# The order of VectorE's steps in the cross-attention of a perceiver kernel, and who adds up the last block's exponentials

## The chip, the cores and the metric

One core of one Trainium2 chip runs the whole program. The time is device microseconds (us) from one execution. Before the change the median of three runs is 1887.72 us, with 1887.4 as the lowest and 1889.46 as the highest.

The engines that matter here are TensorE (PE in the profile, with PEld for its weight loads), VectorE (DVE), ScalarE (ACT), GpSimd (POOL) and SyncE, which issues the DMAs. Each runs its own list of instructions in order and waits on semaphores for the others.

## The reference, cut to what matters

Three residual stages work on x (16 batches of 64 rows of 512). The change touches only the first, the cross-attention with a context of 1601 rows per batch:

```python
q = _split_heads(x @ Wq)            # 16 heads of 32, x after a layer norm
k = _split_heads(y @ Wk)            # y: 16 x 1601 x 512
v = _split_heads(y @ Wv)
attn = jnp.einsum('bhid,bhjd->bhij', q, k) * SCALE
attn = jax.nn.softmax(attn, axis=-1)
out = jnp.einsum('bhij,bhjd->bhid', attn, v)
x = x + out.transpose(0, 2, 1, 3).reshape(b, n, h * d) @ Wp + bp
```

A self-attention and a feed-forward stage follow; neither is changed.

## The kernel before, in words

The cross-attention runs batch by batch: batch 0 written out, batches 1 to 14 in a hardware loop on every engine, batch 15 written out. A batch has a keys phase and a values phase. The 16 heads are four blocks (NBLK) of four heads. Every product of float32 numbers is made in three passes over a high and a low part (three_passes, L113), 12 matmuls each.

**TensorE, keys phase** (batch(), from L942). For each block i it makes four pieces of keys, keys(b, i, 0) to (b, i, 3), and between them the scores of block i - 1 (L916). It also finishes the batch before: weigh(b - 1, i) multiplies that batch's exponentials with its values (L934, 104 small matmuls into small_ps) and spreads the sums of the exponentials by four heads x two halves of matmuls with ones (L938). The single bank small_ps holds one block at a time, so small_read(b - 1, i - 1) makes weigh(b - 1, i) wait until VectorE's output(b - 1, i - 1) has read the block before it.

**TensorE, values phase**. It makes twelve tiles of values, values(b, 0) to values(b, 11), and the scores of block 3 after the first two. Keys and values leave through three PSUM banks in turn (ring). ScalarE empties all key pieces and the odd value tiles, VectorE the even ones (value(b, t), L703). values(b, t) needs the bank of tile t - 3, so tiles 3, 5, 7, 9 and 11 wait for VectorE's copies 0, 2, 4, 6 and 8, and the first key piece of the next batch for copy 10.

**VectorE** (keys_phase, values_phase, L787 to L842) has for each block: largest(b, i, 0) and (b, i, 1), the maxima over the tiles of scores (L724 to L735); row_of_peaks(b, i), twelve small operations in a row that turn them into a row of maxima (L746 to L760); subtract(b, i), which takes that row from the scores in three pieces (L766). Between them stand output(b - 1, i) (a reciprocal at L771 and a product at L775), the copies value(b, t), and low(b + 1, q), the low parts of the next batch's context (L784).

**ScalarE** copies scores out of PSUM (L600), takes the exponentials in three pieces (L606) once subtract has signalled them, and makes the high parts of the context. **GpSimd** adds the 13 tiles of exponentials of a block one after the other (totals, L549 and L555, 12 additions); weigh waits for the last of them (sum_step) ahead of L938.

**Batch 0** has a third part between keys and values. The last 65 context rows of all 16 batches are gathered into nine tiles (LT), whose values TensorE makes at once (left_values(j)). For each tile ScalarE makes a high part (left_high), VectorE a low part (left_low, L707), and the result is copied out by VectorE for even j (left_value, L713) and by ScalarE for odd j. Three slots (LEFT_SLOTS) hold the parts, so the fourth tile waits for left_low(3).

**After batch 15** TensorE weighs its four blocks in banks of their own, with the first output products (out_ahead) between them, and then the block of code ends with a barrier.

Of the kernel before, what the change touches and what calls it, by code (L numbers as in the profile page):

```python
# [13 lines left out]
H, DH = 16, 32  # L14
# [32 lines left out]
TREE_N = 7  # L47
SQ = 32
ROW_N = 9
PIECES = ((0, 4), (4, 8), (8, JT))  # L50
SUMS = JT - 1
LAST_V = (3, 6, 9, VT - 1)
# [341 lines left out]
def cross_attention(nc, x, yT, y_left, v_left, q_dram, o_dram, wv, wp, bp, awq, sh, ident, ones, s_ps):  # L394
# [10 lines left out]
    with ctx:  # L405
# [47 lines left out]
        def last_bank(i):  # L453

            return ring[i] if i < RING else small_ps
# [84 lines left out]

        @block.gpsimd
        def _(pool):
            def totals(b, i):

                done, at = len(PIECES) * (NBLK * b + i), SUMS * (NBLK * b + i)
                acc = fold[:, i, :]
                pool.wait_ge(fold_read, NBLK * b + i + 1)
                pool.wait_ge(exp_ok, done + 1)
                pool.tensor_tensor(acc, prob[:, i, 0, :], prob[:, i, 1, :], ALU.add).then_inc(sum_step, 1)  # L549
                for t in range(2, JT):  # L550
                    if t in (PIECES[1][0], PIECES[2][0]):
                        pool.wait_ge(exp_ok, done + 2 + (t == PIECES[2][0]))
                    pool.wait_ge(sum_step, at + t - 1)
                    m = jtile(t)
                    pool.tensor_tensor(acc[0:m], acc[0:m], prob[0:m, i, t, :], ALU.add).then_inc(sum_step, 1)  # L555

            with pool.Fori(0, B) as b:
                for i in range(NBLK):
                    totals(b, i)
            pool.wait_ge(x_in, 32)  # L560
            for t in range(BIASED):
                if t == ROWS_AHEAD:
                    pool.wait_ge(x_late, 16)
                rows = y.w_raw if t < ROWS_AHEAD else x_rows
                pool.tensor_tensor(rows[:, t, :], rows[:, t, :], y.w_raw[:, ROWS_AHEAD, :], ALU.add)
# [130 lines left out]
        def _(dve):  # L696
# [90 lines left out]
            def keys_phase(b, past):  # L787
                if past:
                    output(b - 1, 0)
                else:  # L790
                    dve.wait_ge(wv_hi, 1)
                    dve.tensor_tensor(sh.wv_s[:, 1], wv_raw, sh.wv_s[:, 0].bitcast(F32),
                                      ALU.subtract).then_inc(wv_lo, 1)
                largest(b, 0, 0)
                largest(b, 0, 1)
                for i in (1, 2):
                    row_of_peaks(b, i - 1)
                    subtract(b, i - 1)
                    largest(b, i, 0)
                    if past:  # L800
                        output(b - 1, i)
                    elif i == 1:
                        for j in range(LEFT_SLOTS):
                            left_low(j)
                    largest(b, i, 1)
                if past:
                    output(b - 1, 3)
                row_of_peaks(b, 2)
                subtract(b, 2)
                if not past:  # L810
                    for j in range(LT):
                        if j % 2 == 0:
                            left_value(j)
                        if j + LEFT_SLOTS < LT:
                            left_low(j + LEFT_SLOTS)

            def values_phase(b, more):
                value(b, 0)
                largest(b, 3, 0)
                value(b, 2)  # L820
                largest(b, 3, 1)
                row_of_peaks(b, 3)
                value(b, 4)
                subtract(b, 3)
                if more:
                    low(b + 1, 0)
                value(b, 6)
                value(b, 8)
                if more:
                    low(b + 1, 1)  # L830
                else:
                    dve.wait_ge(wp_hi, 1)
                    dve.tensor_tensor(y.keep[:, 1], y.w_raw, y.keep[:, 0].bitcast(F32),
                                      ALU.subtract).then_inc(wp_lo, 1)
                    gather(0)
                value(b, 10)
                if more:
                    low(b + 1, 2)
                if more:
                    low(b + 1, 3)  # L840
                else:
                    gather(1)  # L842
# [20 lines left out]
        def _(pe):  # L863
# [57 lines left out]

                reached(pe, o_out, NBLK * b + i + 1)

            def weigh(b, i, at=small_ps):
                block = NBLK * b + i
                if i == 0:
                    pe.wait_ge(act_out, ACT_N * (b + 1))
# [3 lines left out]
                for t in range(JT):  # L931
                    m = jtile(t)
                    for g in range(HB):
                        pe.matmul(at[g * DH:(g + 1) * DH, 0:N], v_sb[0:m, t, (HB * i + g) * DH:(HB * i + g + 1) * DH],  # L934
                                  prob[0:m, i, t, g * N:(g + 1) * N], start=(t == 0), stop=(t == JT - 1))
                pe.wait_ge(sum_step, SUMS * (block + 1))
                for g in range(HB):
                    mm = pe.matmul(at[g * DH:(g + 1) * DH, N:2 * N], ones[:, 0:DH], fold[:, i, g * N:(g + 1) * N],  # L938
                                   start=True, stop=True)
                mm.then_inc(pv_ok, 1)  # L940

            def batch(b, past):  # L942
# [47 lines left out]
            out_ahead(2, range(0, 2))  # L990
            weigh(B - 1, 2, last_bank(2))
            out_ahead(2, range(2, DC))
            weigh(B - 1, 3, last_bank(3))
            out_ahead(3)


# [907 lines left out]
```

## Time and profile before

| what | value |
|---|---|
| runs: median, lowest, highest | 1887.72, 1887.4, 1889.46 us |
| the profiled execution's own time | 1886.98 us |
| its span, first to last instruction | 1885.0 us |
| TensorE busy | 1818.3 us, 96% |
| VectorE busy | 1317.2 us, 70% |
| GpSimd busy | 888.0 us, 47% |
| ScalarE busy | 822.2 us, 44% |
| TensorE clock granted, mean | 0.986 of 2.4 GHz |

Busy time is the union of an engine's instructions. "Idle before" or a bracket behind a row names how long the engine sat idle before that instruction and which instruction of another engine released it. The context stage runs from about 38 to 1560 us of the span: 16 batches of some 91 to 92.6 us each. The granted clock tells which of TensorE's two levels (1.2 or 2.4 GHz) held in a stretch; a mean between them says that both occurred.

### The profile page before, as it was taken

What the parts mean: (1) busy time and instruction counts of PE and PEld (TensorE: products, weight loads), DVE (VectorE), ACT (ScalarE), POOL (GpSimd) and SP (SyncE); (2) the same over time, 40 slices, a digit from 0 to 9 for tenths busy, and PEclk for the clock granted to TensorE, in tenths of its full rate; (3) what the DMA queues carried; (4) which work ended last, traced back from release to release, by engine and by line L of the source; (5) the groups of instructions that cost most, each with busy time, mean ns of one, the idle gap of its engine ahead of it and who ended that gap; (6) DMA issues with size and microseconds to landing.
All of it is one profiled execution on the core that took longest, in us unless ns stands there. A gap on an engine that the chain in (4) does not pass through costs nothing. (4 is left out here: it accounts for less than half of the span.)

```text
span 1885.0 us, 65763 instructions
## 1 busy us (share of the span) xinstructions
PE 1818.3 (96%) x28732; PEld 1573.4 (83%) x28732; DVE 1317.2 (70%) x1942; ACT 822.2 (44%) x982; POOL 888.0 (47%) x830
## 2 busy tenths in 40 slices
PE   8989999999999999999999999999999999999998
PEld 7868888879797979797988888888888877777887
DVE  5855959595959596868686867777676876575265
ACT  4624444454544454444444444444444433344332
POOL 0432727373737373737373636363645463444211
PEclk9989999999999999999999999999999999999999
DMA  7210202020202020202020202020201132033110
GB/s 258 93 52 2 81 3 80 3 80 3 80 3 80 3 80 3 80 3 80 3 80 3 80 3 80 3 80 5 78 10 72 38 109 90 24 91 99 48 56 23
DMA packets 43358, 101.19 MB, mean 54 GB/s; under 512 B 19120, under 2 KB 20656, under 8 KB 42960
## 3 DMA queue, kind: packets, MB, share of 16 engines
q1 hardware_dynamic: 43088, 96.88, 14.7%
q8 instruction: 256, 4.19, 0.9%
q14 instruction: 14, 0.11, 0.0%
HBM read 86.48 MB, written 8.29 MB: 50 GB/s over the span
## 5 line engine op out<-in xcount | busy, mean ns | idle before, releaser
L555 POOL TENSOR_TENSOR fold<-fold,prob 128x256 f32<-128x256 f32 (+1 forms) x704 | 718.4, 1020 | 71.3 <-ACT prob L606 17.0
L113 PE MATMUL ring<-y_parts,w_keep 128*128 128x402 f32 (+1 forms) x3072 | 613.4, 353 | 1.4 <-PEq L191 1.4
L113 PEld LDWEIGHTS ring<-y_parts,w_keep 128*128 128x128 f32 x3072 | 557.2, 190 | 17.0 <-issue 4.9
L113 PE MATMUL ring<-wv_s,y_parts 128*128 128x512 f32 x2304 | 550.5, 396 | 3.3 <-DVE v_sb L703 3.3
L113 PEld LDWEIGHTS ring<-wv_s,y_parts 128*128 128x128 f32 x2304 | 428.4, 188 | 109.6 <-DVE v_sb L703 13.1
L549 POOL TENSOR_TENSOR fold<-prob 128x256 f32<-128x256 f32 x64 | 57.1, 892 | 693.2 <-ACT prob L606 693.2
L575 ACT ACTIVATE k_sb<-ring 128x402 f32<-128x402 f32 (+1 forms) x256 | 129.5, 506 | 414.0 <-PE ring L113 414.0
L766 DVE TENSOR_TENSOR prob<-prob,peak_rows 128x1024 f32<-128x1024 f32 (+1 forms) x192 | 276.6, 1493 | 1.6
L600 ACT ACTIVATE prob<-s_ps 128x1536 f32<-128x1536 f32 (+1 forms) x128 | 200.0, 1562 | 127.5 <-PE s_ps L916 127.5
L731 DVE TENSOR_TENSOR fold<-fold,prob 128x512 f32<-128x512 f32 x192 | 166.6, 868 | 76.5 <-ACT prob L600 72.0
L606 ACT ACTIVATE prob<-prob 128x1024 f32<-128x1024 f32 (+1 forms) x192 | 205.4, 1120 | 0.0
L916 PEld LDWEIGHTS s_ps<-q_sb,k_sb 32*64 32x64 f32 x13312 | 155.9, 130 | 37.5 <-issue 37.2
L916 PE MATMUL s_ps<-q_sb,k_sb 32*64 32x64 f32 x13312 | 173.6, 231 | 0.0
L583 ACT ACTIVATE v_sb<-ring 128x512 f32<-128x512 f32 x96 | 57.5, 599 | 214.5 <-PE ring L113 214.5
L934 PE MATMUL small_ps<-prob,v_sb 128*32 128x64 f32 (+1 forms) x6344 | 112.0, 232 | 33.5 <-DVE o_sb L775 33.5
L934 PEld LDWEIGHTS small_ps<-prob,v_sb 128*32 128x32 f32 (+1 forms) x6344 | 101.3, 118 | 50.9 <-ACT prob L606 36.6
L724 DVE TENSOR_TENSOR fold<-prob 128x512 f32<-128x512 f32 x64 | 52.4, 819 | 130.3 <-ACT prob L600 130.2
L784 DVE TENSOR_TENSOR y_parts<-y_raw,y_parts 128x1608 fp32r<-128x1608 f32 (+1 forms) x60 | 122.9, 2049 | 27.9 <-ACT y_parts L611 27.9
L703 DVE COPY v_sb<-ring 128x512 f32<-128x512 f32 x96 | 64.0, 679 | 78.4 <-PE ring L113 78.4
L611 ACT ACTIVATE y_parts<-y_raw 128x1608 fp32r<-128x1608 f32 (+1 forms) x60 | 92.4, 1540 | 32.8 <-PE ring L113 32.8
L758 DVE COPY peak<-peak 32x8 f32<-32x8 f32 x192 | 61.2, 319 | 6.2
L1309 POOL TENSOR_TENSOR y_parts<-f_raw,y_parts 128x1024 fp32r<-128x1024 f32 x12 | 30.1, 2520 | 73.7 <-ACT y_parts L1345 73.5
(212 smaller groups left out, 1634.5 us busy)
## 6 DMA issues: line engine op xcount, KB each, us to landing
y_raw<-yT SPq DMA_DIRECT2D x48, 804.0 KB, 6.6
y_raw<-yT SPq DMA_DIRECT2D x16, 792.0 KB, 9.1
f_raw<-w_ffn SPq DMA_DIRECT2D x22, 512.0 KB, 3.5
v_sb<-y_left SPq DMA_DIRECT2D x1, 2304.0 KB, 11.2
v_sb<-v_left SPq DMA_DIRECT2D x16, 130.0 KB
p_x<-x SPq DMA_DIRECT2D x4, 512.0 KB, 6.6
q_scratch<-p_x SPq DMA_DIRECT2D x8, 256.0 KB, 2.1
q_sb<-q_scratch SPq DMA_DIRECT2D x16, 128.0 KB, 5.2
```

The source lines that it names most:

```text
L113: mm = pe.matmul(out, left(a, c), right(b, c), start=(c == 0 and n == 0), stop=(c == DC - 1 and n == 2))
L555: pool.tensor_tensor(acc[0:m], acc[0:m], prob[0:m, i, t, :], ALU.add).then_inc(sum_step, 1)
L575: act.activation(k_sb[:, i % 2, at:at + w], bank(unit)[:, 0:w], ACT.Copy).then_inc(act_out, 1)
L600: act.activation(prob[:, i, a:z, :].rearrange("p t (g q) -> p t g q", g=HB), s_ps[:, :, 0:(z - a) * N].rearrange("p g (t q) -> p t g q", q=N),
L606: act.activation(piece(i, n), piece(i, n), ACT.Exp, scale=SCALE).then_inc(exp_ok, 1)
L611: act.activation(y.part(0, q), y.quarter(q), ACT.Copy).then_inc(y_hi_ok, 1)
L703: dve.tensor_copy(v_sb[:, t, :], bank(KEYS + t)[:]).then_inc(dve_out, 1)
L731: dve.tensor_tensor(wide(i), wide(i), prob[:, i, t:t + 2, :], ALU.max).then_inc(tree, 1)
L766: dve.tensor_tensor(piece(i, n), piece(i, n), row(n), ALU.subtract).then_inc(sub_ok, 1)
L784: dve.tensor_tensor(y.part(1, q), y.quarter(q), y.part(0, q).bitcast(F32), ALU.subtract).then_inc(y_lo_ok, 1)
L916: mm = pe.matmul(s_ps[side * N:(side + 1) * N, g, (t - a) * N:(t - a + 1) * N], k_sb[rows, i % 2, at:at + N], q_sb[rows, i, :], start=True ...
L934: pe.matmul(at[g * DH:(g + 1) * DH, 0:N], v_sb[0:m, t, (HB * i + g) * DH:(HB * i + g + 1) * DH], prob[0:m, i, t, g * N:(g + 1) * N], start ...
```

## The change

It has four parts.

1. In the keys phase output(b - 1, 1) and output(b - 1, 2) move from behind largest(b, i, 0) to in front of row_of_peaks(b, i - 1).
2. value(b, 0) moves in front of row_of_peaks(b, 2); value(b, 2) in front of largest(b, 3, 0); value(b, 4) in front of row_of_peaks(b, 3); value(b, 6) and value(b, 8) in front of low(b + 1, 0).
3. In batch 0 the left tiles (left_value, left_low from the fourth tile on) move in front of value(0, 0), row_of_peaks(0, 2) and subtract(0, 2).
4. For the very last block (batch 15, block 3) GpSimd adds only the first seven tiles (six additions for twelve), and TensorE adds the six others in the L938 sums, 24 more small matmuls. GpSimd's loop ends one batch earlier, and batch 15 is written out.

```diff
-                for t in range(2, JT):
+                for t in range(2, tiles):
...
-            with pool.Fori(0, B) as b:
+            with pool.Fori(0, B - 1) as b:
                 for i in range(NBLK):
                     totals(b, i)
+            for i in range(NBLK - 1):
+                totals(B - 1, i)
+            totals(B - 1, NBLK - 1, LAST_SUM)
...
                 for i in (1, 2):
+                    if past:
+                        output(b - 1, i)
                     row_of_peaks(b, i - 1)
                     subtract(b, i - 1)
                     largest(b, i, 0)
-                    if past:
-                        output(b - 1, i)
-                    elif i == 1:
+                    if not past and i == 1:
                         for j in range(LEFT_SLOTS):
                             left_low(j)
                     largest(b, i, 1)
                 if past:
                     output(b - 1, 3)
-                row_of_peaks(b, 2)
-                subtract(b, 2)
-                if not past:
+                else:
                     for j in range(LT):
                         if j % 2 == 0:
                             left_value(j)
                         if j + LEFT_SLOTS < LT:
                             left_low(j + LEFT_SLOTS)
+                value(b, 0)
+                row_of_peaks(b, 2)
+                subtract(b, 2)

             def values_phase(b, more):
-                value(b, 0)
+                value(b, 2)
                 largest(b, 3, 0)
-                value(b, 2)
                 largest(b, 3, 1)
+                value(b, 4)
                 row_of_peaks(b, 3)
-                value(b, 4)
+                value(b, 6)
                 subtract(b, 3)
+                value(b, 8)
                 if more:
                     low(b + 1, 0)
-                value(b, 6)
-                value(b, 8)
-                if more:
                     low(b + 1, 1)
...
-                pe.wait_ge(sum_step, SUMS * (block + 1))
+                pe.wait_ge(sum_step, SUMS * block + summed - 1)
                 for g in range(HB):
-                    mm = pe.matmul(at[g * DH:(g + 1) * DH, N:2 * N], ones[:, 0:DH], fold[:, i, g * N:(g + 1) * N],
-                                   start=True, stop=True)
+                    total = at[g * DH:(g + 1) * DH, N:2 * N]
+                    mm = pe.matmul(total, ones[:, 0:DH], fold[:, i, g * N:(g + 1) * N], start=True,
+                                   stop=(summed == JT))
+                    for t in range(summed, JT):
+                        m = jtile(t)
+                        mm = pe.matmul(total, ones[0:m, 0:DH], prob[0:m, i, t, g * N:(g + 1) * N], start=False,
+                                       stop=(t == JT - 1))
                 mm.then_inc(pv_ok, 1)
...
-            weigh(B - 1, 3, last_bank(3))
+            weigh(B - 1, 3, last_bank(3), LAST_SUM)
```

LAST_SUM is 7, JT 13, SUMS 12. `past` is false in batch 0 alone.

## Rows read from the trace of the kernel before

**Rows 1.** The page's first part: each engine's busy us, share and instructions.
```profile
PE 1818.3 (96%) x28732; PEld 1573.4 (83%) x28732; DVE 1317.2 (70%) x1942; ACT 822.2 (44%) x982; POOL 888.0 (47%) x830
```

**Rows 2.** TensorE's waits, whole span: us in total, times, longest us.
```profile
PE small_ps L934 <- DVE o_sb L775: 33.5, 15, 2.3
PE ring L113 <- DVE left_parts L707: 8.6, 1, 8.6
PE ring L113 <- DVE v_sb L703: 3.3, 16, 0.3
```

**Rows 3.** Timeline, TensorE, batch 6: start, us, instructions, [idle before, releaser].
```profile
667.54 1.66 PE L934 MATMUL small_ps<-prob,v_sb 128*32 128x64 f32 x104 [2.28 <-DVE o_sb L775]
...
671.52 2.95 PE L113 MATMUL ring<-wv_s,y_parts 128*128 128x512 f32 x12
...
699.96 8.61 PE L113 MATMUL ring<-wv_s,y_parts 128*128 128x512 f32 x36 [0.28 <-DVE v_sb L703]
```

**Rows 4.** Timeline, VectorE, batch 6: from row_of_peaks(b, 1) to output(b - 1, 2).
```profile
655.07 0.45 DVE L746 STREAM_TRANSPOSE peak_rows<-fold 128x256 f32<-128x256 f32 x1
...
659.43 4.97 DVE L766 TENSOR_TENSOR prob<-prob,peak_rows 128x1024 f32<-128x1024 f32 x3
...
666.61 0.55 DVE L771 RECIPROCAL rec<-small_ps 128x64 f32<-128x64 f32 x1
```

**Rows 5.** Timeline, TensorE: batch 5's wait; each batch's first L938 group, four of 15.
```profile
160.92 0.30 PE L938 MATMUL small_ps<-fold,ones 128*32 128x64 f32 x8
...
575.12 3.00 PE L934 MATMUL small_ps<-prob,v_sb 128*32 128x64 f32 x104 [2.28 <-DVE o_sb L775]
...
992.10 0.30 PE L938 MATMUL small_ps<-fold,ones 128*32 128x64 f32 x8
...
1083.08 0.30 PE L938 MATMUL small_ps<-fold,ones 128*32 128x64 f32 x8
...
1451.65 0.30 PE L938 MATMUL small_ps<-fold,ones 128*32 128x64 f32 x8
```

**Rows 6.** Stretches: length, busy of PE, PEld, DVE, ACT, POOL, granted clock, DMA share, GB/s.
```profile
575.00:578.30 3.30, 3.18 (x113) 3.01 (x113) 3.20 (x4) 0.27 (x1) 3.06 (x4) 0.50 0.02 5
...
667.50:669.30 1.80, 1.76 (x113) 1.67 (x113) 1.73 (x3) 0.20 (x1) 1.64 (x3) 1.00 0.04 9
```

**Rows 7.** Timeline, TensorE, batch 0: the left tiles and the first value tile.
```profile
82.59 8.37 PE L113 MATMUL ring<-wv_s,left_parts 128*128 128x512 f32 x36
99.55 18.69 PE L113 MATMUL ring<-wv_s,left_parts 128*128 128x512 f32 x72 [8.59 <-DVE left_parts L707]
118.07 2.95 PE L113 MATMUL ring<-wv_s,y_parts 128*128 128x512 f32 x12
```

**Rows 8.** Timeline, VectorE, batch 0: last step of largest(0, 2, 1), first left_value.
```profile
88.14 0.84 DVE L735 TENSOR_TENSOR fold<-fold,prob 65x256 f32<-65x256 f32 x1
...
98.22 0.68 DVE L713 COPY v_sb<-ring 128x512 f32<-128x512 f32 x1
```

**Rows 9.** Timeline, VectorE, batch 6: subtract(b, 2) to low(b + 1, 0).
```profile
677.35 3.89 DVE L766 TENSOR_TENSOR prob<-prob,peak_rows 128x1024 f32<-128x1024 f32 x3
...
688.46 0.45 DVE L746 STREAM_TRANSPOSE peak_rows<-fold 128x256 f32<-128x256 f32 x1
...
692.73 0.65 DVE L703 COPY v_sb<-ring 128x512 f32<-128x512 f32 x1
...
697.48 1.82 DVE L784 TENSOR_TENSOR y_parts<-y_raw,y_parts 128x1608 fp32r<-128x1608 f32 x1
```

**Rows 10.** Timeline, GpSimd: a first addition in batch 6; the last block's additions.
```profile
682.75 1.01 POOL L549 TENSOR_TENSOR fold<-prob 128x256 f32<-128x256 f32 x1 [5.13 <-ACT prob L606]
...
1527.45 14.32 POOL L555 TENSOR_TENSOR fold<-fold,prob 128x256 f32<-128x256 f32 x11
```

**Rows 11.** Timeline, TensorE, after batch 15: in weigh(15, 1), and weigh(15, 3)'s sums.
```profile
1546.65 0.33 PE L934 MATMUL ring<-prob,v_sb 128*32 128x64 f32 x9 [3.00 <-issue]
...
1556.35 0.46 PE L938 MATMUL small_ps<-fold,ones 128*32 128x64 f32 x8
```

More of the change, by code:

```diff
@@ L49 @@
 ROW_N = 9
+LAST_SUM = 7
 PIECES = ((0, 4), (4, 8), (8, JT))
@@ L542, in _, with totals @@
         def _(pool):
-            def totals(b, i):
+            def totals(b, i, tiles=JT):
                 done, at = len(PIECES) * (NBLK * b + i), SUMS * (NBLK * b + i)
@@ L922, in small_read, with weigh @@
                 reached(pe, o_out, NBLK * b + i + 1)
-            def weigh(b, i, at=small_ps):
+            def weigh(b, i, at=small_ps, summed=JT):
                 block = NBLK * b + i
```

## The prediction

> **What bounds the kernel now.** I read the page's busy shares first: TensorE is busy for 1818.3 of 1885.0 us [rows 1], so only its idle time and its slow time can be won, 67 us of the one and an unknown amount of the other. No other engine is over 70%, so what VectorE does matters only where TensorE waits for it. The list of TensorE's waits says where that is [rows 2]: 33.5 us in 15 waits at L934 for VectorE's o_sb (15 batches have a past), 8.6 us in one wait for a left tile's low part, 3.3 us in 16 short waits for a value copy. Together 45.4 us, all of them waits that the change aims at.
>
> The timeline of one batch shows the large one [rows 3]: TensorE is through with its keys at 667.54 - 2.28 = 665.26 and stands until VectorE has written o_sb from output(b - 1, 2). VectorE had small_ps complete long before: it began row_of_peaks(b, 1) at 655.07, went on to subtract at 659.43 and largest(b, 2, 0), and came to the output only at 666.61 [rows 4].
>
> There is a second cost that the waits don't show. In that batch the 104 matmuls behind the wait take 1.66 us; in the batch before, after the same 2.28 us wait, they take 3.00 us [rows 3, 5]. The windows say why: the granted clock was 1.00 in the one stretch and 0.50 in the other [rows 6], so TensorE fell to 1.2 GHz behind its idle time. The starts of the batches' first L938 groups show how often. The 15 starts, from 160.92 to 1451.65, make 14 periods, 1290.73 us in all. Three of them are short, as 1083.08 - 992.10 = 90.98 [rows 5], and eleven are about 92.5. Three short ones come to 273.2 us, so the eleven mean (1290.7 - 273.2) / 11 = 92.5, which is 1.45 us over the short ones' 91.05.
>
> **Output in front of the row of maxima.** Nothing is added or removed, a reciprocal (0.55 us) and a product, some 0.8 us with the gap, change places. output(b - 1, 2) can start at 655.1, when largest(b, 1, 1) ends, and is through at 655.9, while TensorE needs it at 665.3: 9 us of margin. The wait goes whole: 33.5 us. What waits behind it on VectorE is row_of_peaks(b, 1), 0.8 us late; from largest(b, 2, 1) on VectorE is where it was, since the output no longer stands there. subtract(b, 1) ends near 665.2, when ScalarE is about to start that block's exponentials. I cost this at nothing; if that cover is gone it is 0.8 us per batch on the softmax chain, which TensorE reads a phase later. output(b - 1, 1) moves in the same way and had no wait before it.
>
> With the idle time goes the slow clock behind it: 11 x 1.45 = 15.9 us. The bounds are 0 (the clock falls for another reason) and 15.9; I take 15.9, since the slow matmuls stand directly behind the wait, and the clock of the rest of such a batch is 1.00.
> The Trainium skill (TensorE: Matmul & The Clock Gate, "A second HAM failure mode: psum-queue depth-cycling") warns that small idle gaps between groups of matmuls can be enough to make the clock drop again and again. By that rule the short waits that remain could keep the clock loss, and the sum would be 15.9 us smaller. In the trace a wait of 0.28 us [rows 3] has no slow matmuls behind it; 2.28 us has, in 11 of 14 batches.
>
> **Value copies between VectorE's steps.** TensorE will come to its value tiles 2.3 us earlier than before, and VectorE is where it was, so each copy's margin must be worked out. TensorE's tile 9 started at 699.96 after 0.28 of waiting [rows 3]; without that and the 2.28 it starts at 697.4. The tiles are 8.61 / 3 = 2.87 us or slightly less apart, so tile 7 starts at 691.7, tile 5 at 686.1, tile 3 at 680.4, tile 11 at 703.0, and the next batch's keys at 705.9.
> Copies cost 0.65 to 0.7 us each. subtract(b, 2) started at 677.35 and took 3.89 [rows 9]; copy 0 now stands before row_of_peaks(b, 2), so it is done about 673.5 (tile 0 ended at 671.52 + 2.95 = 674.5 before, at 672.1 now). Margin for tile 3: 7 us. Copy 2 follows subtract at about 682.5, margin 3.6 for tile 5. largest(b, 3) ends at 688.4, as before [rows 9], since two copies stood ahead of that point in both orders; copy 4 is done at 689.1, margin 2.6 for tile 7. row_of_peaks(b, 3) takes until copy 4's old place at 692.7 plus one copy: copy 6 done at 694.1, margin 3.3 for tile 9. In the old order copy 6 stood behind the subtraction and a low part (697.48 plus 1.82) and was done near 700, which is the 0.28 us of waiting. subtract(b, 3) and copy 8 are done at 699.0, margin 4 for tile 11. Two low parts (1.8 and 2.0) and copy 10 end at 703.5, margin 2.4 for the next keys. So the 16 short waits go too, 3.3 us, and no new one takes their place.
> The prices depend on GpSimd: subtract takes 4.97 us [rows 4] in a stretch in which GpSimd adds and 3.89 [rows 9] in one in which it stood idle for 5.13 us [rows 10]. If the whole difference of 1.1 us fell on subtract(b, 2), and as much again on largest(b, 3, 0), copy 4 would use 2.2 of its 2.6 us. I take no loss, and 0.5 us x 15 = 7.5 us as a wide end.
> The Trainium skill (SBUF — State Buffer, "Who interferes with whom") says that a VectorE instruction with two inputs in SBUF and a GpSimd instruction that reads SBUF block one another for a whole instruction. That speaks against packing the steps closer; the trace agrees in direction, with the 1.1 us above for three instructions.
>
> **Left tiles first.** TensorE finished three left tiles at 82.59 + 8.37 = 90.96 and waited 8.59 us for left_low(3) [rows 7]. VectorE was free of largest(0, 2, 1) at 88.98 but did row_of_peaks and subtract first and came to the left tiles at 98.22 [rows 8]. In the new order left_value(0) and left_low(3) are done by 90.3 to 90.9, as TensorE asks. The six later tiles took 118.07 - 99.55 = 18.5 us; at the pace of the first three (8.37 / 3, a little under 2.8 with overlap, 2.72) they take 16.3. So 8.6 plus 2.2 = 10.8 us. The 2.2 us are again slow matmuls behind an idle stretch. The displaced row_of_peaks(0, 2) and subtract(0, 2), 9 us, now run after copy 0, and their exponentials come no earlier than ScalarE's place for them, behind both score copies; hidden. SyncE's stores of the left tiles follow 11 us earlier, and copy 4's wait for them is met by then.
>
> **The last block's sums.** GpSimd's additions end at 1527.45 + 14.32 = 1541.8 [rows 10]; TensorE asks for them at 1556.35 [rows 11], 14.6 us later. There is no wait to remove: dropping six additions wins nothing on TensorE's path. TensorE pays 24 more small matmuls; 104 take 1.66 us, so 24 take 0.4 us, and at the slow clock (3.00 per 104) 0.7. They lie on the end of the block and count. GpSimd's bias additions start earlier, but wait for their rows. I take +0.4. Even with TensorE 4.6 us earlier (next point) the cover is 10 us.
>
> **A term that may move either way.** In weigh(15, 1) TensorE stood 3.00 us for "issue" [rows 11], no engine being named. The instructions ahead of it are the same and keep their places relative to TensorE, so I leave it. It could go or come elsewhere: 3 us, with a slow clock some 4.5, either way.
>
> **Sum.** 33.5 + 15.9 + 3.3 + 10.8 - 0.4 = 63.1 us. A wait that goes also gives back a little overlap between matmul groups, up to 0.07 us each, 1 us. So 64.1 off the profiled execution's own 1886.98, which is 1822.9; the median lies 0.7 above that execution, so 1823.6. TensorE is late next in nothing: it becomes the bound of the whole stage, with batches of 91.05 - 2.56 = 88.4 us.
>
> **The rivals.**
> A: the clock's loss stays, or moves to some other place in a batch. For it: in 3 of 14 batches the same wait left the clock alone, so the wait isn't the whole cause. Against it: the slow matmuls always start at the wait. Time 1823.6 + 15.9 = 1839.5.
> B: a value copy becomes late after all, by contention with GpSimd, and TensorE waits 0.5 to 1.5 us per batch: 1831 to 1846. For it: margins of 2.4 to 2.6 us on copies 4 and 10. Against: VectorE's order of work up to those points is the old one and only TensorE moves.
> C, slower than before: VectorE becomes the bound in the values phase. All of its steps from output(b - 1, 3) to copy 10 stand nearly without a gap. If packing made them late by 7 us, copy 4 would be 4.4 us late in each batch and the clock would fall behind it (1.45); from 4 us of new waiting per batch on, the gain of 64 us over 16 batches is gone. At 7 us: 15 x 5.9 = 88, minus 64, so about 1911. For it nothing in the rows but the contention; it would need six times the 1.1 us.
> D: the change doesn't do what it says, because weigh(b - 1, 3) finds another wait at the same place. Its exponentials and sums belong to the batch before and were complete 40 us earlier, so I see none. Time about 1885.
>
> **How the numbers follow.** Forecast as summed, with 0 to 7.5 us of small new waits or the issue term either way: 1817 to 1829, chance 0.77. A 0.07, B 0.10, C 0.04, D 0.02. The range takes the forecast and the nearer half of B: 1816 to 1836, with A's 1839.5 left out. A measurement can tell about 0.2% (3.8 us) from no change; forecast, A and B are all faster than that, 0.94; D is the same, 0.02; C slower, 0.04.
>
> **What would show it.** Right: TensorE's wait at L934 for o_sb is gone from the list, all batches have equal periods near 88.4 us with clock 1.00, left tiles run without a gap and end near 107, the waits for value copies vanish, and the last L938 group has 32 matmuls. Wrong: a wait for v_sb over 0.3 us (B or C), windows at 0.50 inside batches (A), a new gap ahead of weigh(b - 1, 3) under another name (D).

## The result, and the profile after

The changed kernel takes 1815.94 us (median of four runs, 1812.55 to 1816.66) beside 1887.56 for the kernel before; the ratio is 0.9618, with a 95% interval of 0.9601 to 0.9634. It is faster by 71.6 us. The forecast was 1823.6 in a range of 1816.0 to 1836.0. The direction and most terms of the sum held; the time came out 7.7 us below the forecast and 0.06 us below the range. Two of the four executions (1816.54 and 1816.66) lie inside the range, so by how little it was missed says nothing; the 7.7 us are what has to be explained.

The page of the kernel after, its busy times (as [rows 1]). TensorE is busy for 99% of the span, which was 1885.0 us and is 1813.5:

```profile
span 1813.5 us, 65800 instructions
PE 1795.0 (99%) x28780; PEld 1561.4 (86%) x28780; DVE 1304.9 (72%) x1942; ACT 827.1 (46%) x982; POOL 898.7 (50%) x824
```

TensorE's waits after, the longest two (the second is at the very start). None is left at the places of [rows 2]; what was 45.4 us there is nothing here. The first is the gap in weigh(15, 1) that stood in [rows 11] as 3.00 us:

```profile
PE ring L938 <- issue: 2.3, 1, 2.3
PE p_t L388 <- POOL ident L244: 1.5, 1, 1.5
```

Timeline of TensorE after: batch 0's left tiles and values (answering [rows 7]), the first small matmuls of batches 1 and 15, and the last piece of keys with the fourth weighing in batch 6 (answering [rows 3]). There is no bracket, that is no idle time, in a batch, and weigh(b - 1, 3) starts where the keys end:

```profile
82.12 24.76 PE L114 MATMUL ring<-wv_s,left_parts 128*128 128x512 f32 x108
106.72 2.95 PE L114 MATMUL ring<-wv_s,y_parts 128*128 128x512 f32 x12
...
115.15 28.07 PE L114 MATMUL ring<-wv_s,y_parts 128*128 128x512 f32 x120
...
147.55 1.66 PE L938 MATMUL small_ps<-prob,v_sb 128*32 128x64 f32 x104
...
628.61 2.48 PE L114 MATMUL ring<-y_parts,w_keep 128*128 128x402 f32 x12
631.01 1.66 PE L938 MATMUL small_ps<-prob,v_sb 128*32 128x64 f32 x104
...
1380.43 1.66 PE L938 MATMUL small_ps<-prob,v_sb 128*32 128x64 f32 x104
```

The first weighings of batches 1 and 15 are 1232.88 us apart, 14 periods of 88.06 us; they were 1290.73 apart [rows 5]. A stretch of one period after, with the columns of [rows 6], shows TensorE busy throughout and the clock at 1.00, 2.4 GHz:

```profile
540.00:628.00 88.00, 88.00 (x1632) 77.54 (x1623) 67.50 (x99) 42.58 (x46) 49.37 (x48) 1.00 0.13 45
```

**Where the 71.5 us of span went.** The same landmarks in both timelines, in order:

| stretch of TensorE's work | before, us | after, us | gained |
|---|---|---|---|
| start to the first keys | 38.39 | 37.95 | 0.4 |
| to the first value tile of batch 0 | 79.68 | 68.77 | 10.9 |
| to the first weighing, weigh(0, 0) | 41.37 | 40.83 | 0.5 |
| 14 periods | 1290.73 | 1232.88 | 57.9 |
| batch 15 from weigh(14, 0) to the next stage | 109.91 | 109.34 | 0.6 |
| the rest | 324.92 | 323.73 | 1.2 |

VectorE after, in batch 6's values phase (answering [rows 9]). Copies 0, 4 and 10 are shown; they stand where the new order puts them, and only copy 10 waits, for TensorE:

```profile
638.75 0.68 DVE L707 COPY v_sb<-ring 128x512 f32<-128x512 f32 x1
...
654.67 0.68 DVE L707 COPY v_sb<-ring 128x512 f32<-128x512 f32 x1
...
668.76 0.69 DVE L707 COPY v_sb<-ring 128x512 f32<-128x512 f32 x1 [0.77 <-PE ring L114]
```

### The profile page after: what moved, and what is told of

Read it like the earlier page. It is cut to its first block and busy times, and to the rows that moved or that the text cites. A ratio compares the mean times of both kernels' runs of the same rounds, so it can differ in the third digit from the quotient of the medians.

```text
span 1813.5 us, 65800 instructions
## 1 busy us (share of the span) xinstructions
PE 1795.0 (99%) x28780; PEld 1561.4 (86%) x28780; DVE 1304.9 (72%) x1942; ACT 827.1 (46%) x982; POOL 898.7 (50%) x824
## 3 DMA queue, kind: packets, MB, share of 16 engines
q8 instruction: 256, 4.19, 1.0%
## 5 line engine op out<-in xcount | busy, mean ns | idle before, releaser
L556 POOL TENSOR_TENSOR fold<-fold,prob 128x256 f32<-128x256 f32 x698 | 705.8, 1011 | 55.2
L114 PEld LDWEIGHTS ring<-y_parts,w_keep 128*128 128x128 f32 x3072 | 551.6, 188 | 15.6 <-issue 2.3
L550 POOL TENSOR_TENSOR fold<-prob 128x256 f32<-128x256 f32 x64 | 80.7, 1261 | 622.1 <-ACT prob L610 621.9
L770 DVE TENSOR_TENSOR prob<-prob,peak_rows 128x1024 f32<-128x1024 f32 (+1 forms) x192 | 261.6, 1415 | 1.6
L735 DVE TENSOR_TENSOR fold<-fold,prob 128x512 f32<-128x512 f32 x192 | 172.9, 901 | 79.7 <-ACT prob L604 73.9
L610 ACT ACTIVATE prob<-prob 128x1024 f32<-128x1024 f32 (+1 forms) x192 | 210.8, 1125 | 7.4 <-DVE prob L770 5.1
L938 PEld LDWEIGHTS small_ps<-prob,v_sb 128*32 128x32 f32 (+1 forms) x6344 | 91.5, 110 | 16.6 <-issue 16.6
L938 PE MATMUL small_ps<-prob,v_sb 128*32 128x64 f32 (+1 forms) x6344 | 101.4, 220 | 0.0
```

The costliest lines, as they stand in the source:

```text
L114: mm = pe.matmul(out, left(a, c), right(b, c), start=(c == 0 and n == 0), stop=(c == DC - 1 and n == 2))
L610: act.activation(piece(i, n), piece(i, n), ACT.Exp, scale=SCALE).then_inc(exp_ok, 1)
L735: dve.tensor_tensor(wide(i), wide(i), prob[:, i, t:t + 2, :], ALU.max).then_inc(tree, 1)
L770: dve.tensor_tensor(piece(i, n), piece(i, n), row(n), ALU.subtract).then_inc(sub_ok, 1)
```

## Experiments

Each kernel was timed in turns with the kernel before. The profiled executions serve for what lies below a few us.

| kernel | median, us | ratio to before, 95% interval |
|---|---|---|
| changed kernel, second time | 1815.19 | 0.963 (0.9617 to 0.9643) |
| outputs alone | 1868.85 | 0.9906 (0.9889 to 0.9922) |
| copies alone | 1877.37 | 0.9952 (0.9936 to 0.9969) |
| left tiles alone | 1875.84 | 0.9948 (0.9932 to 0.9965) |
| changed, output(b - 1, 2) behind | 1869.38 | 0.9911 (0.9887 to 0.9934) |
| changed, output(b - 1, 2) between | 1835.2 | 0.9728 (0.9712 to 0.9744) |
| changed, copies 6 and 8 back | 1885.38 | 0.9993 (0.9983 to 1.0003) |
| changed, last sums whole on GpSimd | 1813.69 | 0.9623 (0.961 to 0.9636) |
| changed, last sums by tile | 1813.23 | 0.9622 (0.9609 to 0.9635) |
| last sums whole, late rows of x held | 1810.55 | 0.9607 (0.9594 to 0.962) |

### The outputs alone

The kernel before with part 1 of the change only:

```diff
                 for i in (1, 2):
+                    if past:
+                        output(b - 1, i)
                     row_of_peaks(b, i - 1)
                     subtract(b, i - 1)
                     largest(b, i, 0)
-                    if past:
-                        output(b - 1, i)
-                    elif i == 1:
+                    if not past and i == 1:
                         for j in range(LEFT_SLOTS):
                             left_low(j)
```

> The kernel before with only output(b - 1, 1) and (b - 1, 2) moved ahead of row_of_peaks. Theory of the forecast's sum taken part by part: the 33.5 us of waits and 15.9 us of slow clock belong to this part alone, so about 1887.6 - 50 = 1837. Rival, the wait moves: TensorE now comes 2.35 us earlier to value tile 9 while VectorE's copy 6, still behind subtract and a low part, is done at the same time as before (about 700 in batch 6, wanted at 697.4). Then TensorE waits some 2.6 us per batch for v_sb in place of o_sb, the clock may fall behind that wait too, and the time is 1880 to 1890.

It took 1868.85, 18 us less than before: neither number. TensorE's waits in this kernel:

```profile
PE ring L113 <- DVE v_sb L703: 31.5, 45, 1.4
PE ring L113 <- DVE left_parts L707: 8.6, 1, 8.6
```

The 33.5 us at o_sb are gone, and 31.5 - 3.3 = 28 us have come back as waits for value copies, three per batch (45 in all) in place of one. The timeline of TensorE in one batch shows them, in front of value tiles 3, 7 and 9:

```profile
676.90 9.30 PE L113 MATMUL ring<-wv_s,y_parts 128*128 128x512 f32 x39 [1.37 <-DVE v_sb L703]
688.84 5.83 PE L113 MATMUL ring<-wv_s,y_parts 128*128 128x512 f32 x24 [0.56 <-DVE v_sb L703]
694.85 8.61 PE L113 MATMUL ring<-wv_s,y_parts 128*128 128x512 f32 x36 [0.18 <-DVE v_sb L703]
```

So the wait did move, as the rival had it, though it begins at copy 0 and not at copy 6. The tile 9 waits start at 603.85 and 694.85 in two neighbouring batches: a period of 91.00, the same as a short period of the kernel before. What was gained is the slow clock: the periods are 91.0 to 91.2 us now. The stall comes in three pieces, of which the longest is 1.37 us, and the clock stays at 1.00:

```profile
600.00:690.00 90.00, 87.90 (x1613) 76.49 (x1612) 67.06 (x99) 42.35 (x46) 47.15 (x48) 1.00 0.12 44
```

### The value copies alone

```diff
+                if past:
+                    value(b, 0)
                 row_of_peaks(b, 2)
...
-                value(b, 0)
+                if isinstance(b, int) and b == 0:
+                    value(b, 0)
+                value(b, 2)
                 largest(b, 3, 0)
-                value(b, 2)
                 largest(b, 3, 1)
+                value(b, 4)
                 row_of_peaks(b, 3)
-                value(b, 4)
+                value(b, 6)
                 subtract(b, 3)
+                value(b, 8)
                 if more:
                     low(b + 1, 0)
-                value(b, 6)
-                value(b, 8)
-                if more:
                     low(b + 1, 1)
```

> The kernel before with only the value copies moved (batch 0 keeps its copy 0 and left tiles in the old places). As the forecast priced it, by TensorE's idle time in front of tile 9 (3.3 us in 16 waits): 1884. Rival, the true price is what the values phase took longer: tiles 2 to 11 took 28.60 us in batch 6 before and 27.91 after the whole change, 0.69 us for a listed wait of 0.28, and 28.44 for a listed 0.17. Then some 0.55 us x 16 = 9 us: 1879. The waits for o_sb stay at 2.28 us.

1877.37, or 9.5 us less than the 1886.86 beside it (0.0048 of it is 9, with 6 to 12 in the interval), where the waits list only 3.3 us. In its own trace the waits for v_sb are gone and those for o_sb are 33.6 us as before. The rival price holds: late copies that TensorE's matmul rows put at 0.17 to 0.28 us in a batch cost it about 0.55. The weight loads of the kernel before show more of it; in the list of PEld's waits (same columns as [rows 2]) the same cause has 13.1 us, not 3.3, and 28 waits, not 16. Here is that line, then the timeline of the weight loads in batch 5 (tiles 7 and 9) and batch 6 (tile 9):

```profile
PEld ring L113 <- DVE v_sb L703: 13.1, 28, 0.7
```

```profile
602.99 5.40 PEld L113 LDWEIGHTS ring<-wv_s,y_parts 128*128 128x128 f32 x24 [0.25 <-DVE v_sb L703]
608.99 2.15 PEld L113 LDWEIGHTS ring<-wv_s,y_parts 128*128 128x128 f32 x10 [0.60 <-DVE v_sb L703]
...
699.96 8.18 PEld L113 LDWEIGHTS ring<-wv_s,y_parts 128*128 128x128 f32 x36 [0.71 <-DVE v_sb L703]
```

In 12 of the 16 batches there are two late copies, 4 and 6, and the first of them (0.24 us at tile 7) doesn't show in the matmul rows at all; tiles 2 to 11 take 0.53 us too long there. In the four others only copy 6 is late, and they take 0.69 us too long for a listed 0.28. Together that is 12 x 0.53 + 4 x 0.69 = 9.1 us, an estimate from the lengths of these phases, and it agrees with the measured 9.5. Part of the difference to the listed time is how the rows are drawn: two matmul rows in a row overlap (82.12 + 24.76 = 106.88, where the next starts at 106.72), so a row's idle time leaves out some 0.16 us. That the rest is lost overlap of weight loads with matmuls is argued, not shown.

### The left tiles alone

```diff
-                row_of_peaks(b, 2)
-                subtract(b, 2)
                 if not past:
                     for j in range(LT):
                         ...
+                    value(b, 0)
+                row_of_peaks(b, 2)
+                subtract(b, 2)

             def values_phase(b, more):
-                value(b, 0)
+                if not (isinstance(b, int) and b == 0):
+                    value(b, 0)
```

> The kernel before with only batch 0's left tiles ahead of copy 0, row_of_peaks(0, 2) and subtract(0, 2). Both theories: 8.6 us of waiting and 2.2 us of slow matmuls go, 10.8 us: 1876.8, with the third and fourth left tile without a gap and TensorE's first value tile near 107 us. Rival: the 2.2 us stay because the clock falls elsewhere in batch 0: 1879.

1875.84 beside 1886.86: 11.0 us, with 6.6 to 12.8 in the interval. The wait for left_parts is gone from the list. In the changed kernel's trace the nine tiles run without a gap from 82.12 to 106.72, 24.6 us for the 35.5 of [rows 7], which is 10.9.

### output(b - 1, 2) put back in the changed kernel: long and short wait

Behind largest(b, 2, 0), its old place:

```diff
-                    if past:
+                    if past and i == 1:
                         output(b - 1, i)
                     row_of_peaks(b, i - 1)
                     subtract(b, i - 1)
                     largest(b, i, 0)
+                    if past and i == 2:
+                        output(b - 1, i)
```

> The changed kernel with output(b - 1, 2) put back behind largest(b, 2, 0), all else kept. Theory: the wait for o_sb is back with its full price, 15 x 2.3 us and slow matmuls behind it in most batches, so 1815.9 + 35 + 16 = 1867. Rival, the clock's loss had another cause: the wait is back but not the slow matmuls, 1851. If both the wait and the loss stayed away, the wait would have been the value copies' doing: 1816.

In the middle of largest(b, 2, 0), between its two operations:

```diff
-                    if past:
+                    if past and i == 1:
                         output(b - 1, i)
                     row_of_peaks(b, i - 1)
                     subtract(b, i - 1)
-                    largest(b, i, 0)
+                    largest(b, i, 0, (lambda: output(b - 1, i)) if past and i == 2 else None)
```

> The changed kernel with output(b - 1, 2) put between the two operations of largest(b, 2, 0), so that TensorE's wait for o_sb is there but shorter: subtract ends at 664.4 on batch 6's old clock, the first operation takes 1.2, the output is through at 666.4, TensorE asks at 665.3, so some 1.2 us of waiting. Theory, the clock falls only behind the long wait: 15 x 1.3 = 19 us, 1835, clock 1.00 in every batch. Rival, any wait at this place makes it fall in most batches: 1835 + 16 = 1851.

The long wait gave 1869.38, 53 us over the changed kernel; the theory had 51. The short one gave 1835.2, 19 us over it, where the theory had 19. TensorE's timeline with the output behind, four of the 15 waits:

```profile
284.12 3.00 PE L940 MATMUL small_ps<-prob,v_sb 128*32 128x64 f32 x104 [2.30 <-DVE o_sb L779]
...
651.89 2.36 PE L940 MATMUL small_ps<-prob,v_sb 128*32 128x64 f32 x104 [2.28 <-DVE o_sb L779]
...
927.64 1.66 PE L940 MATMUL small_ps<-prob,v_sb 128*32 128x64 f32 x104 [2.27 <-DVE o_sb L779]
...
1018.01 3.00 PE L940 MATMUL small_ps<-prob,v_sb 128*32 128x64 f32 x104 [2.28 <-DVE o_sb L779]
```

then, with the output between, its wait in the list, one in the timeline, and all weighing matmuls of the stage (shortest, median and longest duration in ns, first and last start):

```profile
PE small_ps L940 <- DVE o_sb L781: 16.6, 15, 1.2
```

```profile
639.37 1.66 PE L940 MATMUL small_ps<-prob,v_sb 128*32 128x64 f32 x104 [1.15 <-DVE o_sb L781]
```

```profile
L940 PE MATMUL small_ps<-prob,v_sb x6344: 217/219/244, 148.0 to 1503.4; 128*32 128x64 f32 x183, 65*32 65x64 f32 x16
```

The reader is to see three things. With 2.28 us of idle time the 104 matmuls behind it take anything from 1.66 to 3.00 us, and from batch to batch the number falls slowly from 3.00 to 1.66 and jumps back; in the kernel with the copies alone it does the same, and in the kernel before it rises in three to five batches to 3.00 and falls back to 1.66. What a slow batch loses doesn't change with it: from wait to wait it is 91.9 us both behind a 3.00 and behind a 1.93, and 90.4 only behind a 1.66 (1018.01 - 927.64 = 90.37). A short slow stretch starts a little earlier or later behind the wait, so the loss falls on the 104 matmuls or on the keys behind them. In the kernel before, the 104 matmuls at 205.04 take only 1.88 us, but the 12 key matmuls behind them 3.63 for the usual 2.43; the granted clock is 0.50 there from 207 to 209 us. The forecast's "the slow matmuls always start at the wait" is right only to within about a microsecond.

With 1.15 us not one of 6344 matmuls took over 244 ns; in the kernel before, the longest of the same 6344 took 316. So the slow clock is the long wait's, as the forecast had it. The wait alone doesn't settle it for a single batch, though: behind 2.28 us the clock held in 3 of 14 batches before, and why is open. The wait of batch 15 is shorter, 1.58 us before, and had no slow matmuls either:

```profile
1495.07 1.66 PE L934 MATMUL small_ps<-prob,v_sb 128*32 128x64 f32 x104 [1.58 <-DVE o_sb L775]
```

### Copies 6 and 8 put back in the changed kernel

```diff
                 row_of_peaks(b, 3)
-                value(b, 6)
                 subtract(b, 3)
-                value(b, 8)
                 if more:
                     low(b + 1, 0)
+                value(b, 6)
+                value(b, 8)
+                if more:
                     low(b + 1, 1)
```

> The changed kernel with value copies 6 and 8 back behind subtract(b, 3) and low(b + 1, 0), all else kept. By the forecast's margins copy 6 is then done near 700.1 for a tile 9 that could start at 697.3: a wait of 2.8 us per batch, which with its hidden 0.3 to 0.4 us costs 16 x 3.1 = 50 us, 1866, and up to 16 us more if the clock falls behind it (1882): nearly the whole gain, from the order of one copy. Rival, copies have slack enough in either place and only the earlier ones (0 and 2) matter, as in the run with the outputs alone: 1816 to 1820.

1885.38, no different from the kernel before: two copies in their old places take the whole gain back. TensorE's waits and one of them in its timeline:

```profile
PE ring L114 <- DVE v_sb L707: 40.6, 16, 2.8
```

```profile
508.97 10.18 PE L114 MATMUL ring<-wv_s,y_parts 128*128 128x512 f32 x36 [2.70 <-DVE v_sb L707]
518.99 4.56 PE L114 MATMUL ring<-y_parts,w_keep 128*128 128x402 f32 x24
```

The 2.70 us are the 2.8 that the margins gave. The 36 matmuls behind them take 10.18 us for the 8.61 of [rows 3]: the clock falls here too (0.50 from 510 to 512 us), and so it does behind all 15 waits of over 2 us. The price is what the forecast's rival C had given for late copies (from 4 us per batch on, idle and slow time together, the 64 us are gone), but C's cause, a VectorE that has too much to do, isn't at work: here one copy stands in the wrong place.

Set beside the outputs alone, this run tells the most about the clock. It has the outputs, the left tiles and copies 0, 2 and 4 early, and is still 16.5 us slower than the kernel that has only the outputs early (1885.38 and 1868.85, from two comparisons whose kernels before differ by 0.9). There a batch's stall came as 1.37, 0.56 and 0.18 us and the clock stayed at 1.00; here it is one piece of 2.70 us.

### Who adds up the last block

GpSimd adds all 13 tiles again (batch 15 still written out):

```diff
-            totals(B - 1, NBLK - 1, LAST_SUM)
+            totals(B - 1, NBLK - 1)
...
-            weigh(B - 1, 3, last_bank(3), LAST_SUM)
+            weigh(B - 1, 3, last_bank(3))
```

> The changed kernel with GpSimd adding all 13 tiles of the last block again, TensorE only spreading the sum. As the forecast priced the change's fourth part (24 matmuls at 104 per 1.66 us): 0.4 us faster than the changed kernel. Theory from the trace after: the last sums took from 1483.75 to 1486.42, 2.7 us, for 0.4 before, so 2.3 us faster, 1813.6, and no wait for GpSimd, whose additions end some 10 us ahead. Rival, part 4 was needed because TensorE now asks earlier: a wait for GpSimd appears in front of the last sums, and it is slower.

TensorE's added matmuls tile by tile, four heads in turn:

```diff
-                    for t in range(summed, JT):
-                        m = jtile(t)
-                        mm = pe.matmul(total, ones[0:m, 0:DH], prob[0:m, i, t, g * N:(g + 1) * N], start=False,
-                                       stop=(t == JT - 1))
+                for t in range(summed, JT):
+                    m = jtile(t)
+                    for g in range(HB):
+                        mm = pe.matmul(at[g * DH:(g + 1) * DH, N:2 * N], ones[0:m, 0:DH],
+                                       prob[0:m, i, t, g * N:(g + 1) * N], start=False, stop=(t == JT - 1))
```

> The changed kernel with the last block's 24 added matmuls issued tile by tile, four heads in turn, instead of head by head. Theory: six matmuls one after another on one head's 32 columns go one by one (0.08 to 0.1 us each), four heads in turn go as in the weighing (104 in 1.66 us), so the last sums take 0.6 to 0.7 us and the kernel is 2 us faster than the changed one. Rival, the number of matmuls with ones is what costs (weights loaded anew for each): still 2.7 us and no difference.

The medians are 1813.69 and 1813.23 beside 1815.19 for the changed kernel in the same comparison: 1.5 and 2.0 us less, with intervals that overlap, so the verdict rests on the traces. The last sums and what follows them on TensorE; with the sums whole:

```profile
1483.40 0.32 PE L943 MATMUL small_ps<-fold,ones 128*32 128x64 f32 x8
1483.64 3.06 PE L987 MATMUL s_ps<-w_keep,y_parts 128*128 128x512 f32 x12
```

in the changed kernel (first and last rows of the sums):

```profile
1483.75 0.28 PE L943 MATMUL small_ps<-fold,ones 128*32 128x64 f32 x2
...
1485.62 0.87 PE L947 MATMUL small_ps<-prob,ones 65*32 65x64 f32 x14
1486.42 3.04 PE L987 MATMUL s_ps<-w_keep,y_parts 128*128 128x512 f32 x12
```

and tile by tile:

```profile
1480.88 0.30 PE L942 MATMUL small_ps<-fold,ones 128*32 128x64 f32 x8
1480.99 0.85 PE L947 MATMUL small_ps<-prob,ones 128*32 128x64 f32 x48
1481.77 3.04 PE L987 MATMUL s_ps<-w_keep,y_parts 128*128 128x512 f32 x12
```

The sums take 0.24 us whole, 2.67 head by head and 0.89 tile by tile (start of the sums to the start of L987). The clock is 1.00 in all three. So part 4 of the change costs 2.4 us here, of which 1.8 is the order of the loops, and it removes no wait: with the sums whole there is none for GpSimd. The Trainium skill (TensorE: Matmul & The Clock Gate, "The mechanism" of Part 3) says that matmuls at different 32 x 32 positions of the array run at the same time; its section "What picks the tile position" says that the column position follows from where the output starts. The trace agrees: four heads in turn go 3 times as fast as six matmuls in a row on one head's 32 columns.

Part 4 gives 1.0 us of it back in the next stage, where the forecast didn't look. There VectorE normalises four tiles (L1102) and GpSimd follows with additions (L1296), released by the first. Timelines of the two engines in the changed kernel:

```profile
1497.04 2.88 DVE L1102 TENSOR_SCALAR y_raw<-x_sb,co_mv,co_ve 128x512 f32<-128x512 f32 x4
```

```profile
1498.04 5.52 POOL L1296 TENSOR_TENSOR x_sb<-x_sb,sa_chain 128x512 f32<-128x512 f32 x4 [4.49 <-DVE y_raw L1102]
```

and with the sums whole:

```profile
1494.27 3.83 DVE L1102 TENSOR_SCALAR y_raw<-x_sb,co_mv,co_ve 128x512 f32<-128x512 f32 x4
```

```profile
1494.97 5.53 POOL L1296 TENSOR_TENSOR x_sb<-x_sb,sa_chain 128x512 f32<-128x512 f32 x4 [4.17 <-DVE y_raw L1102]
```

With part 4 GpSimd starts 1.00 us behind VectorE, without it 0.70, and the four tiles take 2.88 or 3.83 us. The single operations of the two timelines say where the 0.95 us lie: one that starts ahead of GpSimd's first addition takes 0.55 us, one that starts behind it 1.50. With part 4 three of the four start ahead of it (the fourth at 1498.41), without it two (the third at 1495.19). Six kernels of this study have part 4 and six haven't, the kernel before among them, and they fall into these two groups without exception (6.8 or 7.7 us for the eight tiles at that line). Why GpSimd starts later is open; its code ahead of that point is longer by what batch 15 written out adds, but so it is in the two kernels with whole sums on GpSimd. Net, part 4 costs 1.4 us by the traces; the medians say 1.5, a difference near their noise.

### The gap inside weigh(15, 1)

The last sums whole, and the 1.25 MB load of x held back until weigh(15, 1) is through:

```diff
             sp.wait_ge(out_lo, len(BY_QUARTER))
+            sp.wait_ge(pv_ok, NBLK * (B - 1) + 2)
             sp.dma_start(x_rows[:, ROWS_AHEAD:], ...
```

> e1 with the last rows of x (the 1.25 MB load behind out_lo) issued only after weigh(15, 1). Theory: the 2.3 us gap for issue in the middle of weigh(15, 1), and the slow matmuls behind it (4.60 us for 12 instead of about 3.0), come from instructions of TensorE that are fetched over DMA engines busy with that load (DMA share 1.02 ahead of the gap in the kernel before); then both go and it is 3.5 to 4 us faster than e1. Rival, the gap is the sequencer's own and stays at the same matmul: no difference to e1, or slower if the load then ends too late for the next stage.

1810.55 beside 1813.69 without the hold, 3.1 us less; the intervals of the ratios (0.9594 to 0.962 and 0.961 to 0.9636) overlap a little, but all five executions with the hold (1810.19 to 1811.25) are faster than all five without it (1812.83 to 1814.92). The trace is plain. Without the hold, windows over the 96 matmuls before the gap and over the gap:

```profile
1471.20:1472.70 1.50, 1.50 (x96) 1.38 (x96) 0.04 (x1) 1.43 (x1) 1.42 (x3) 1.00 1.00 384
1472.70:1475.30 2.60, 0.04 (x6) 0.01 (x2) 2.60 (x1) 0.00 (x0) 2.60 (x3) 1.00 0.30 102
```

with the hold, a window over all 112:

```profile
1470.40:1472.10 1.70, 1.70 (x113) 1.61 (x112) 0.29 (x1) 1.38 (x1) 1.62 (x3) 1.00 0.00 0
```

With the DMA engines full (share 1.00, 384 GB/s) TensorE stops for 2.56 us in the midst of a run of small matmuls, waiting for no other engine; with them idle it doesn't stop. That there is no gap without the load is shown. That the load makes it by keeping instructions from being fetched is the likely way (the profile has an instruction queue among its DMA queues, 4.19 MB), but only argued. Nor does the load always cost that much: ahead of the same nine matmuls the gap was 2.28 to 3.00 us in nine traces with the load, 0.97 in the one with copies 6 and 8 back and 0.21 in the one with the sums tile by tile, where the DMA engines were just as full (share 1.02). What decides its length is open.

This is the fastest version of all, 4.6 us below the changed kernel.

## Why the prediction was right or wrong, point by point

**What bounds it.** Right. TensorE's idle and slow time was all there was to win: its busy share went from 96% to 99% and every wait of [rows 2] is gone.

**Output in front of the row of maxima.** Right in size inside the whole change. The changed kernel with the output behind costs 53.4 us more, for 50.4 forecast (33.5 of waits, 15.9 of slow clock, 1 of overlap); 12 of its 14 batches were slow, by about 1.55 us each, for the forecast's 11 by 1.45, which is most of the rest. Left open in the forecast was how far this part hangs on the next: alone it brought 18 us, since the wait went to the copies.

**The slow clock.** Right, and rival A fell: the loss of 15.9 us went with the long wait, stayed away with a 1.15 us wait (16.6 us of waits, 19 us of time, clock 1.00), and came back with the long one. The Trainium skill (TensorE: Matmul & The Clock Gate, "A second HAM failure mode: psum-queue depth-cycling") warns of small gaps between groups of matmuls. No run here bears that out: the gaps of 0.18 to 1.37 us that the runs with the outputs alone and with the output between have in every batch left the clock at 1.00.

**Value copies between VectorE's steps.** The positions were right to within 0.8 us: relative to the first value tile (635.00 in batch 6), copy 4 was the furthest behind, ending at 655.35 when the forecast's 689.1 comes to 654.9, and copy 8 was 0.8 us early. The term of the sum was wrong, and this is the step that failed: "So the 16 short waits go too, 3.3 us". The mechanism, waits that go when the copies come earlier, was right; the term was sized by TensorE's idle time as its matmul rows show it, and that isn't what the waits cost. The copies alone brought 9.5 us (6 to 12 in the interval), and in the two timelines values 2 to 11 took 28.60 us before in batch 6 (679.96 to 708.56) and 27.91 after (115.15 to 143.06 in batch 0), 0.69 for a listed 0.28. At 0.53 us in twelve batches and 0.69 in four the term is 9 to 10 us, 6 more than forecast. The period says the same: a short one of 91.05 less 2.56 us of listed waits is 88.5 (the forecast writes 88.4), and 88.06 was measured. The rows that would have warned of it were there, in the list of the weight loads' waits, 13.1 us for the same cause; as a price they are too high.

**Left tiles first.** Right, 10.9 us for 10.8.

**The last block's sums.** Right that there was no wait to remove and that this part costs time; the size was wrong, 2.3 us (2.67 - 0.39) for 0.4, with 1.0 us given back in a stage that the forecast didn't look at. The forecast took the price of 104 matmuls that go four heads in turn for 24 that go six in a row on one head. This error lay on the other side and hid part of the first.

**The issue term** gave 0.7 us (3.00 to 2.34), inside its bounds. That a load fills the DMA engines ahead of it (share 1.02 from 1542.0 to 1543.6 us in the kernel before) could have been read in the windows.

**The sum again.** 64.1 forecast, 71.6 between the two profiled executions (1886.98 and 1815.34). Copies +6, last sums -1.9, issue +0.7, start of the program +0.4, the stages behind +1.2, and about 1 more in the 16 batches than these terms name. The 1.2 us are part 4's doing, 1.0 of them at the normalisation shown above: with the last sums whole, the stages behind take 324.9 us again. The start is scatter: in the twelve traces of this study the first keys begin between 37.95 and 38.90 us, and the changed kernel has the lowest of them. The last 1 us is not explained. Without the copies' 6 us the measured time would have been near 1822, inside the range; the other errors largely cancel, which is luck.

**The rivals.** None of them came. B and C need late copies, and the margins held; whether packing the steps closer could make VectorE the bound, as C had it, no run shows. Put back in its old place, copy 6 cost what C had put on late copies.

## What to carry to other kernels

When the bounding engine waits in two places on one helper, don't price the waits one by one: work out when each of the helper's results is ready and wanted in the new order, since an early release at one place brings the next request forward by the same amount. Here the outputs alone gave 18 us, the copies alone 9.5, the left tiles 11, and all together 71.6. And price a short wait of TensorE by the length of its phase with and without it: here the matmuls' idle time was too low a price (3.3 us for 9.5) and the weight loads' too high (13.1). Where part of a stall had to stay, it was cheaper here in several short pieces than in one long one.

## What the runs showed of the hardware that was not expected

- A wait of 0.28 us in front of a 512-column group of matmuls, 0.71 by the weight loads, cost 0.69 us; where the matmul rows showed 0.17, the weight loads had waited twice (0.25 and 0.60) and the cost was 0.53.
- The same idle time of 2.28 us had slow matmuls behind it in 11 or 12 of 14 batches, 1.45 to 1.55 us lost each time, and the place of the slow stretch moved slowly from batch to batch; idle times of 1.58, 1.37 and 1.15 us had none.
- A VectorE operation that started ahead of GpSimd's first addition took 0.55 us, one that started behind it 1.50. So four of them took 3.83 us when GpSimd started 0.70 us behind VectorE, and 2.88 when it started 1.00 behind.
- Six small matmuls in a row with the same 32 output partitions take some 0.09 to 0.1 us each; with four groups in turn 32 took 0.89 us together.
- With a load that fills the DMA engines (1.25 MB, share 1.00) TensorE stopped for 0.21 to 3.00 us (2.3 to 3.0 in nine of eleven traces) in a dense run of small matmuls, without any semaphore; without the load it didn't.
